# A three-block transformer layer on one core: value mixing in four column tiles, a projection of 12 products, and new orders of work on every engine

## The reference, cut to what matters

```python
x = x + xattn(layernorm(x), ctx, Wq, Wk, Wv, Wo, bo)   # 16 heads of 64, 128 context rows of 96 per batch entry
x = x + attn(layernorm(x), Wp, bp, Wv, Wo)             # 16 heads, similarity from 5 sigmoid paths, causal
x = x + ffn(layernorm(x), Wq, bq, K1, K2, W_up, W_down)
# xattn
scores = einsum('bhid,bhjd->bhij', q, k) * scale
attn = softmax(scores)
out = einsum('bhij,bhjd->bhid', attn, v)               # v = context @ Wv
return out.reshape(...) @ Wo + bo
# ffn: two top-10 lists of 32 keys, the 10 best sums of both, softmax over them, gelu(x @ w_down) * scores @ w_up
```

## Time and profile before

| | us |
|---|---|
| median of 3 runs | 1133.36 (1131.19 to 1134.92) |
| the profiled run, its own time | 1133.51 |
| span of its profile | 1131.7 |
| TensorE, ACT, DVE, POOL busy share of the span | 89%, 85%, 78%, 73% |
| granted TensorE clock, mean | 0.97 of 2.4 GHz |

### The profile page before, as it was taken

One profiled execution on the slowest core, in us unless ns is written; L12 is line 12 of the kernel. 1 busy time (PEld: TensorE's weight loads), 2 busy tenths in 40 slices (PEclk: granted clock), 3 DMA queues, 4 the chain that ended last, 5 costly groups with the idle time before them and its releaser, 6 DMA issues.

```text
span 1131.7 us, 34471 instructions
## 1 busy us (share of the span) xinstructions
PE 1009.9 (89%) x11656; PEld 771.8 (68%) x11656; DVE 883.9 (78%) x2941; ACT 960.1 (85%) x2251; POOL 824.9 (73%) x871
## 2 busy tenths in 40 slices
PE   3789899999999999999999999999999999999755
PEld 3666677777766777776677777766776777667433
DVE  2447788888888888888888888888888888888763
ACT  2579899999999999999999999999998999998642
POOL 0137777777987777788777777887777779777755
PEclk9999999999999999999999999999999999999865
DMA  6000000000000000000000000000000000000000
GB/s 158 13 13 12 14 15 4 16 16 16 17 13 16 11 9 16 16 16 14 16 16 7 13 16 17 16 14 16 17 4 16 16 16 15 13 14 7 4 3 6
DMA packets 36684, 18.79 MB, mean 17 GB/s; under 512 B 13632, under 2 KB 36256, under 8 KB 36512
## 3 DMA queue, kind: packets, MB, share of 16 engines
q1 hardware_dynamic: 32832, 14.91, 4.8%
q10 hardware_dynamic: 3680, 1.67, 0.6%
HBM read 14.47 MB, written 2.10 MB: 15 GB/s over the span
## 4 chain that ended last, share of the span: by engine, by line
DVE 29%; PE 27%; POOL 17%; issue 14%; ACT 10%; SPq 1%; DVEq 1%; POOLq 0%; DMA 0%; ACTq 0%
POOL wsum L1111 10%; PE psXT L386 9%; ACT p L698 6%; DVE mw L1003 6%; POOL feat L1095 5%; DVE cand L974 5%; DVE top L942 4%; DVE best L969 3%; DVE best L979 3%; PE psXT L351 3%; PE psXT L441 3%; PE psF L571 2%; PE psXT L370 2%; ACT am L737 2%; DVE us L954 1%
## 5 line engine op out<-in xcount | busy, mean ns | idle before, releaser
L1111 POOL TENSOR_TENSOR wsum<-wsum,mw 128x1024 f32<-128x1024 f32 x192 | 451.7, 2353 | 165.0 <-DVE mw L1003 159.4
L1003 DVE SCALAR_TENSOR_TENSOR mw<-psF,cut,ew 128x1024 f32<-128x1024 f32 x256 | 325.8, 1281 | 56.8 <-ACT ew L788 53.0
L788 ACT ACTIVATE ew<-psF,lnz 128x1024 f32<-128x1024 f32 x256 | 288.3, 1127 | 13.3 <-PE psF L571 10.2
L698 ACT ACTIVATE p<-psXT,negmax 128x128 f32<-128x128 f32 x512 | 182.2, 387 | 2.5 <-DVE negmax L876 2.5
L571 PE MATMUL psF<-sel,usT 128*128 128x512 f16 x512 | 157.0, 389 | 23.4 <-DVE mw L1003 20.4
L351 PE MATMUL psXT<-cT,q 96*128 96x128 f32 x1024 | 140.4, 281 | 22.8 <-ACT p L698 18.2
L351 PEld LDWEIGHTS psXT<-cT,q 96*128 96x128 f32 x1024 | 128.4, 194 | 42.9 <-ACT p L698 33.8
L1062 POOL TENSOR_TENSOR p<-p,rrow 128x512 f32<-128x512 f32 x128 | 131.2, 1035 | 19.0 <-DVE rrow L885 19.0
L386 PE MATMUL psXT<-pT,c 128*96 128x512 f32 x256 | 134.2, 611 | 0.8 <-ACT pT L604 0.8
L404 PE MATMUL psXT<-vo,uT 96*128 96x128 f32 x1024 | 121.2, 277 | 0.0
L698 ACT ACTIVATION_READ_ACCUMULATOR p<-psXT,negmax 128x1 f32 x512 | 117.2, 229 | 0.0
(11 more groups left out here) (132 smaller groups left out, 2265.1 us busy)
## 6 DMA issues: line engine op xcount, KB each, us to landing
cT<-cT_dram SPq DMA_DIRECT2D x32, 96.0 KB, 2.0
c<-c_dram SPq DMA_DIRECT2D x32, 96.0 KB, 2.0
x<-x_dram SPq DMA_DIRECT2D x32, 64.0 KB, 2.2
xr<-x_dram SPq DMA_DIRECT2D x32, 64.0 KB, 1.8
y_dram<-y SPq DMA_DIRECT2D x32, 64.0 KB, 2.4
wqT<-wqT_dram SPq DMA_DIRECT2D x1, 512.0 KB, 5.9
wo<-wo_dram ACTq DMA_DIRECT2D x1, 512.0 KB, 9.8
wdT<-wdT_dram SPq DMA_DIRECT2D x1, 512.0 KB, 6.6
```

Source lines behind the costliest of these rows:

```text
L698: ins = act.activation(p[:, k, i, :], bank[BANK[f"x.s{k}"]][:, i * M:i * M + M], ACT.Exp, bias=negmax[:, k, i:i + 1], accum_out=rowsum[:, ...
L788: done(f"e.x{h}", act.activation(ew[:, h % NEW, :], bank[BANK[f"e.s{h}"]], ACT.Exp, bias=lnz[:, t % 4, h:h + 1]))
L1003: done(f"e.w{h}", dve.scalar_tensor_tensor(out=mw[:, h % NMW, :], in0=bank[BANK[f"e.s{h}"]], scalar=cut[:, t % 4, h:h + 1], in1=ew[:, h % ...
L1111: done(f"e.a{h}", pool.tensor_tensor(wsum[:, t % 2, :], mw[:, 0, :] if h == 1 else wsum[:, t % 2, :], mw[:, h % NMW, :], ALU.add))
```

## The change

Five things are altered.

1. **Mixing.** `y.m{k}` is no longer one product with 96 output rows and 512 columns. Of each four heads three go to output partitions 0 to 95 in three column tiles of 32 (384 columns each), and the fourth head's 96 rows are laid in column tile 96 to 127 as three pieces of 128 columns. So four heads take three blocks of 128 rows by 64 columns, with no empty row; a step has six products, each on 32 columns of the array.
2. **Projection.** `uT` and `vo` follow: 12 blocks of 128 rows in place of 16 of 96. `y.out` has 12 products. The copies `y.u*` have 128 x 384 in place of 96 x 512. `setup_vo` lays `vo` out in the same way.
3. **Orders and banks.** All tables are new, with the waits for banks that follow from them. `e.w6` stands ahead of `k.top` and no more behind `k.cand`; `e.s6` with it ahead of the mixing; lags of `x.q3`, `x.x2`, `x.e2`, `t.path`, `k.z`, `k.lnz`, `e.s2`, `e.x2`, `e.add` and others rise by one, which moves them over the seam of the cyclic list and leaves them at about their place.
4. **Loads.** Tile 1 of x is loaded seventh of all on SP; the weights follow in the order of their use, all on SP but `wkT`; `awo` takes 2 loads in place of 16.
5. **Setup.** `setup_keys` on DVE comes at `t.div` of tile 0 and its last part (`setup_down`) at `k.top` of tile 0. Some semaphores are merged.

```diff
-                    done(f"y.m{k}", pe.matmul(bank[BANK[f"y.m{k}"]][0:CD, :], c0[:, t % 2, k // 2, :], pT[:, k, :],
-                                              start=True, stop=True))
+                    probs = pT[:, k, :].rearrange("m (g j q) -> m g j q", g=2, j=4)
+                    to = bank[BANK[f"y.m{k}"]][:, 0:6 * N].rearrange("c (g j q) -> c g j q", g=2, j=3)
+                    for j in range(3):
+                        cols = c0[:, t % 2, k // 2, 32 * j:32 * j + 32]
+                        pe.matmul(to[32 * j:32 * j + 32], cols, probs[:, :, 0:3, :], start=True, stop=True,
+                                  tile_position=(0, 32 * j))
+                        mm = pe.matmul(to[96:128, :, j, :], cols, probs[:, :, 3, :], start=True, stop=True,
+                                       tile_position=(0, 96))
+                    done(f"y.m{k}", mm)
...
-                for h in range(XH):
-                    mm = pe.matmul(out, uT[:, h, :, :].rearrange("c b q -> c (b q)"), vo[:, h, :],
-                                   start=False, stop=(h == XH - 1))
+                for i in range(XH3):
+                    mm = pe.matmul(out, uT[:, i, :, :].rearrange("c b q -> c (b q)"), vo[:, i, :],
+                                   start=False, stop=(i == XH3 - 1))
...
-                    to_sb(eng, f"y.u{k}", uT[:, 8 * (k % 2):8 * (k % 2) + 8, k // 2, :],
-                          bank[BANK[f"y.m{k}"]][0:CD, :].rearrange("c (h q) -> c h q", h=8))
+                    to_sb(eng, f"y.u{k}", uT[:, 6 * (k % 2):6 * (k % 2) + 6, k // 2, :],
+                          bank[BANK[f"y.m{k}"]][:, 0:6 * N].rearrange("c (i q) -> c i q", i=6))
...
             load_ct(0)
             load_c(0)
-            load_xr(0)
+            load_x(1)
+            sp.dma_start(wvT[:], by_chunk(a["wvT"])).then_inc(own["wvo_load"], 16)
+            sp.dma_start(wo[:], by_chunk(a["wo"])).then_inc(own["wvo_load"], 16)
...
+            for r in range(2):
+                sp.dma_start(awo[N * r:N * r + N, :], by_rank[r]).then_inc(own["tree_load"], 16)
...
-    4, "k.top": 4, "x.low": 2, "k.split": 4, "e.w7": 5, "y.res": 3, "k.cand": 4, "e.w6": 5, "k.z": 4, "e.add":
+    "e.w5": 5, "x.stats": 1, "k.low": 4, "e.w6": 5, "k.top": 4, "k.split": 4, "x.low": 2, "e.w7": 5, "y.res": 3,
```

More of the change, by code:

```diff
@@ L149, in run @@
                         once[name]()
-                    if 0 <= t < NT and not (t == 0 and name in begun):
+                    if 0 <= t < NT and (name, t) not in begun:
                         steps[name](t)
@@ L237, in _ @@
             sp.dma_start(wup[:], by_chunk(a["wup"])).then_inc(own["expert_load"], 16)
[L238 to L243, removed]
+            run(steps, SP_ORDER, begun=(("ld.x", 0), ("ld.x", 1), ("ld.ct", 0), ("ld.c", 0), ("ld.xr", 0)))
             sp.wait_ge(s["st.y"], 16 * NT)
@@ L507, in keys_turn @@
             def keys_turn(t):
-                after(pe, "y.res", t + 1)
-                at_ends(pe, "t.csb", t)
+                pe.wait_ge(s["k.shift"], t + 1)
                 if t == 0:
-                    pe.wait_ge(own["tree_load"], 16 * 21)
+                    pe.wait_ge(own["tree_load"], 16 * 7)
                 pe.wait_ge(s["k.split"], t + 1)
@@ L551, in step @@
                     elif h == 2:
[L552 to L553 removed]
+                        pe.wait_ge(s["e.gelu"], t + 1)
                     elif h == 3:
@@ L1029, in _ @@
                                                    op0=ALU.mult, op1=ALU.subtract)
-                ins.then_inc(own["qk_split"], 1)
-            run(steps, DVE_ORDER, begun=("x.stats",), once={DVE_BIAS: setup_bias, DVE_KEYS: setup_keys})
+                ins.then_inc(own["split_done"], 1)
+            run(steps, DVE_ORDER, begun=(("x.stats", 0),), once={DVE_BIAS: setup_bias, DVE_KEYS: setup_keys, DVE_DOWN: setup_down})
         @block.gpsimd
@@ L1122 @@
 PE_ORDER = {
-    "e.s1": 5, "x.s3": 3, "e.s0": 5, "t.fturn": 4, "x.s1": 3, "e.s3": 5, "t.sim": 4, "e.wturn": 6, "e.s4": 5,
-    "x.p0": 3, "t.mix": 4, "e.s5": 5, "x.p2": 3, "t.cturn": 4, "y.m0": 3, "t.out": 4, "x.p3": 3, "y.m2": 3,
-    "x.p1": 3, "e.s7": 5, "y.m3": 3, "k.turn": 4, "y.m1": 3, "x.turn": 2, "k.key": 4, "e.hid": 4, "y.out": 3,
-    "e.s6": 5, "x.q1": 2, "x.q0": 2, "k.kturn": 4, "x.q2": 2, "e.out": 6, "x.s2": 2, "t.turn": 3, "t.pv": 3,
-    "e.s2": 4, "x.s0": 2, "x.q3": 2,
[3 rows of a table added]
+    "x.turn": 2, "e.hid": 4, "y.out": 3, "x.q0": 2, "x.q1": 2, "k.kturn": 4, "e.out": 6, "x.q2": 2, "t.turn": 3,
@@ L1164 @@
 DVE_BIAS = "x.x2"
-DVE_KEYS = "y.res"
+DVE_KEYS = "t.div"
+DVE_DOWN = "k.top"
 def kernel(**inputs):
```

201 lines of the change are left out of this document (103 added, 98 removed), and 16 rows, old and new, of tables (ACT_ORDER, BANK, PE_ORDER).

## The result

| | before | after |
|---|---|---|
| median | 1133.15 us (1131.19 to 1134.92) | 1120.13 us (1116.67 to 1122.43) |
| the profiled run, its own time | 1133.51 | 1117.91 |
| its span | 1131.7 | 1116.0 |
| start of the first and the last L945 (L963 after) | 77.7, 1086.6 | 70.5, 1073.7 |

The ratio is 0.988 (0.985 to 0.992). The forecast was 1094, so the sign was right and the gain was 13 us where 39 were expected. It ended close to rival (a), 1119 us.

The account below looks back on a forecast made before the run. Bound: a latency loop through the engines, 32.52 us. Less 0.5 and 0.65, plus 0.1 for mode changes, gives 31.5, -32 us over 31 iterations; start -7.5; span 1092, time 1094 us (1076 to 1112 at 65%; range 1066 to 1126).

Parts of the forecast that it names:

- rival (a): Loop: a wait for a mask or a copy takes the gain back, adding 0.8 us an iteration; 1119 us; chance 16%.
- The start: Before the loop: tile 1 of x, loaded seventh, is there before it is asked for; -7.5 us.
- the wait of `k.cand` for `k.shift`: DVE, first half of the loop: DVE gets to `k.cand` early and waits 0.4 us for ACT's `k.shift`.
- the wait ahead of `k.top`: DVE: idle 1.31 us before `k.top` in the kernel before; no wait over 0.3 us there would show the forecast right.
- POOL's wait: POOL: its 5.0 us wait for a mask in each iteration would be gone.
- a mixing step: TensorE: column tiles run abreast, so a step takes 0.7 us for 0.9 in the kernel before.
- Rival (b): TensorE: column tiles don't run abreast over 128 rows and the kernel is slower, 1158 or 1238 us; chance 11%.
- The price of a change of mode: TensorE: about 0.1 us for each change of tiling mode, four around the mixing; 0.1 us added to the loop.
- The drain: After the loop: POOL's 7 sums and the last experts keep their order; 0, give or take 2 us.
- the term for the first half of the loop: DVE, `k.top` to the end of `t.path`: 13.55 us, -0.5 from 14.02, with bounds -1.2 and 0.
- The second half of the loop: From the end of `t.path` through all engines to `k.top`: 17.85 us for 18.50, -0.65, bounds -1.1 to 0.1.
- the 15.8 that I had named as the sign: Second half: `k.turn` starting more than 15.8 us after `t.path` ends would show the forecast wrong there.

Follow-up runs that it names:

- xroot_moved: The changed kernel with `x.root` moved on POOL from before `e.a7` to behind `x.n2`, so that `e.a7` runs earlier: 1100.39 us.
- cut_reduce: The changed kernel with the sum `cut` on DVE formed by a reduction of one operand in place of a two-operand addition: 1105.06 us.
- es1_twice: The changed kernel with the two products of `e.s1` on TensorE done twice, the repeat being useless work: 1111.32 us.
- w3_first: The changed kernel with the copy `x.w3` put ahead of `x.x0` on DVE: 1121.55 us.
- before_pool_long: The kernel before with two spare additions on POOL ahead of `e.a6`, each reading both halves of `wsum`: 1189.58 us.
- fturn_first: xroot_moved with `t.fturn` put ahead of `e.s0` on TensorE: 1129.84 us.
- before_packed: The kernel before, with its own orders, banks and loads, but with the packed mixing and the projection of 12 products: 1136.90 us.
- cut_and_xroot: The changed kernel with both the `cut` as a reduction of one operand and `x.root` moved behind `x.n2` on POOL: 1101.84 us.

## Why the prediction was right and where it was wrong

**The bound** was named rightly: a loop of latency through all engines, counted 31 times, and no engine full. The start (7.2 for 7.5 us), the first `x.q` (13.93 for 14), the wait of `k.cand` for `k.shift` (0.48 for 0.4), the wait ahead of `k.top` gone, POOL's wait gone, and a mixing step of 0.66 to 0.71 for 0.7 came as written. Rival (b) is out: the wide passes start 0.03 us apart. By the rate in the Trainium skill, page "TensorE: Matmul & The Clock Gate", section "Measured speedup vs the span model", a step would be 0.8, an estimate; the rows here say less. The price of a change of mode came too: the first packed pass starts 0.52 us after a pair of products (548.65, L590) that takes 0.43. The drain was 2.8 us shorter, where I had 0, give or take 2.

**The step that failed first is the term for the first half of the loop**: "From table load to the end of `t.path` I get 4.3 + 4.7 + 2.2 = 11.2". The 4.7 for `k.cand` took the durations of its instructions from the kernel before, where POOL stood still beside them. I listed POOL's 5.0 us wait as something that goes, and didn't ask what POOL would run then, and beside what. `k.cand` and its `cut` took 533.37 - 528.33 = 5.04 and the end of `t.path` came at 11.43; without the stall it comes at 11.06 (xroot_moved). The stall is worth 0.22 to 0.36 us an iteration (cut_reduce, xroot_moved), 7 to 11 us.

**A term was missing**: the granted clock. I costed the shorter `y.out` and mixing as time off the path, and the clock at nothing. TensorE's busy time fell from 1009.9 to 984.7 us, it stood 1.55 us in two waits ahead of the turn of the features, and ten times the granted clock fell: 8.4 us by the iterations, 8.8 by es1_twice. The falls came with the stall: the copy `x.w3` stands behind the `cut` in DVE's queue, so the first of these waits of TensorE is 1.18 us with the stall, 1.02 in cut_reduce and 0.87 in xroot_moved, and in these two there is no fall. So the stall cost 15 to 20 us in all. es1_twice shows that filling 0.43 us of the idle time ends the falls with the stall in place, w3_first that moving it doesn't, and before_pool_long that they appear in the kernel before too when TensorE is made to wait. But idling more is not enough: fturn_first, whose TensorE stands 3.3 us an iteration in waits over 0.15 us (2.6 in after), has no fall from 100 to 1062 us, nor has before_packed from 126 to 1068 us, with 21 us less work on TensorE than the kernel before. What precisely sets them off stays open.

**The second half of the loop was mis-sized, by as much**: 18.33 for 17.85, and 0.48 x 31 = 15 us. In the iteration shown above, to `t.fturn` 3.22 (3.0), to the end of the similarity 4.39 (4.35), to the end of `t.mix` 2.78 (2.65), to `t.cturn` 0.85 (1.0), to `t.out` 1.27 (1.2), to `k.turn` 3.50 (3.5), to `k.top` 2.32 (2.15). `k.turn` starts 16.0 us after `t.path` ended, over the 15.8 that I had named as the sign. The largest miss is the first, where `e.s0` waits for a mask, as rival (a) said; fturn_first shows that it can't simply be taken out, and the other misses were not tested. The half stays within the bounds given for it (-1.1 to 0.1), but near the wrong end: -0.17.

**The sum.** A quiet iteration took 32.11 us for 31.5. The stall is 0.36 of it and the second half 0.48; the rest of the first half came out 0.13 under its 13.55 (13.42 in xroot_moved), and the 0.1 for changes of mode lies within the measured stretches. Times 31 that is 11 + 15 - 4 - 3 = 19 us. With falls 8, start 0.3 and drain -2.8 it makes 24.5, and the profiled span is 1116.0 for 1092. With the stall and the falls gone the iteration is still 31.75 (xroot_moved), 0.25 over the forecast. Rival (a), with 16%, named 1119 us, and that 1120 was measured is mostly luck: waits behind masks do stand in the second half, but the 15 to 20 us of the stall and its falls were no part of it. That stall isn't a wait for a semaphore, and so it stands in no list of waits. It shows as a longer duration.

The best version measured is the changed kernel with `x.root` moved, 1100.4 us, 2.8% under the kernel before; with the other form of the `cut` as well (1101.8) it is the same within the noise.

## What to carry to other kernels

A duration read from a trace holds for the neighbours that it had: when a change fills an engine's wait, look what the other engines run there, above all small DVE instructions on SBUF beside long POOL ones, and compare durations line by line after the change, since such a stall is in no list of waits. Work on TensorE that is off the path isn't free to take away or to add: adding 0.43 us of it ended the falls of the clock. Look at the granted clock of single iterations, and at whether iterations are of two lengths. And measure a part of a change with the disturbances removed: packing looked worth nothing (1121.5 against 1120.1 us), and against the kernel without the stall it is worth 0.78 us an iteration.

## What the hardware showed that I had not expected

- A DVE sum of 128 x 8 takes 0.17 us alone, and 0.43, 0.54 or 1.35 us when a POOL addition of 128 x 1024 runs beside it; it ends with POOL's instruction. As a reduction of one operand it takes 0.17 beside the same addition.
- A `tensor_scalar` of 128 x 8 had the rest of the same wait (0.33 for 0.17).
- 0.43 us of useless products an iteration made the kernel 8.8 us faster in the median, with the granted clock at 1.00 all through the loop.
- In the profiled runs of xroot_moved and cut_and_xroot the clock was granted from 40.2 us on instead of 17.5, though TensorE was busy without a gap from 14 to 30 us; these runs took 1110 us, most others of the same kernels 1099 to 1102.
